# Cutting features as 128k + p in place of 4p + k in a chain of an RNN, a low-rank layer and an LSTM

## The chip, the cores and the metric

One NeuronCore of a Trainium2 chip runs the kernel. TensorE (PE) multiplies, VectorE (DVE) and ScalarE (ACT) do elementwise work, GpSimd (POOL) some reductions, SyncE (SP) issues DMAs; ScalarE issues a few too. The metric is the time of one execution on the device in microseconds.

## What is computed

Four layers with residuals, for 32 sequences (B) of 128 steps (T) and 512 features (D), in fp32. All layers but the second and fourth treat time steps alone; those two are recurrent, with 512 states.

```python
def reference(x, cond, ...):                      # x (32, 128, 512), cond (32, 512)
    ys = cond / sqrt(512)                         # layer 0: modulated linear
    d = rsqrt((ys * ys) @ (w0 * w0) + 1e-8)
    x = x + ((x * ys[:, None]) @ w0) * d[:, None]
    h = cond                                      # layer 1: RNN over t
    for t: h = tanh(h @ Wh1 + x[:, t] @ Wx1 + b1); x[:, t] += h
    ae = layernorm(cond) * ln_g + ln_b            # layer 2: low-rank hyper-network, rank 8
    xw = gelu(ae @ w1 + hb1) @ w2 + hb2           # 8192 values: a (512, 8) and b (512, 8)
    x = x + x @ (base + a @ b.T)
    h, c = cond, 0                                # layer 3: LSTM over t
    for t:
        i, f, o, g = split(x[:, t] @ Wx3 + b3 + h @ Wh3)
        c = sigmoid(f) * c + sigmoid(i) * tanh(g)
        h = sigmoid(o) * tanh(c)
        y[:, t] = x[:, t] + h
    return y
```

## The kernel before

**Data.** Features stand on the 128 partitions, in KC = 4 chunks (index k), with time and batch along the free side. Which feature stands where is set by `by_row` (L296): partition p, chunk k holds feature 4p + k, so each partition of a 512 x 512 weight is one stretch of 8 KB in memory. x, cond, b1 and the output come from arrays in the order 128j + p; `by_block` (L300) picks one j of them, and four DMAs, each to or from 32 partitions, move one tile (`load_x` L352, the stores L411, `condT` L612, `b1T` L374). On chip `columns` (L303) takes every fourth column where a chunk of output features is wanted: for the stationary operands of the dense products (`chunks` L1321), for the sources of the transposes in the LSTM step (L1034, L1037) and in a few operations of the start. `wh1` alone is put in order when it is split (`wh1_high` L495, `wh1_low` L808).

**Precision.** Each fp32 operand is split into a high and a low fp16 part (ScalarE's `high`, L477, and VectorE's `low`, L756), and a product is three fp16 products.

**The gates.** `wx3` and `wh3` come from memory with the columns of a row in the order (chunk j of 128 state features, gate g, feature in the chunk). A gate matmul (`gates_x` L1378, `gates_h` L1386) has a 128 x 32 stationary operand (state or input, all 32 sequences) and 512 moving weight columns; j = 0 to 3 go to four groups of 32 columns of the array, and to PSUM partitions 32j to 32j + 31. A step of the LSTM has 48 from x and 48 from h. The state leaves its elementwise work as 128 (j, b) x 128 features and is turned in blocks of 32 x 32 by VectorE (L1034 for the scaled fp16 copy that TensorE waits for, L1037 for the fp32 one).

**Order.** Every engine's order is written out by hand and kept by semaphores. Tiles have 4 time steps; the LSTM runs LAG = 2 tiles behind the RNN. TensorE's main loop (L1475) runs 30 rounds of four LSTM steps (`lstm`, `gates_x`), four RNN steps (`rnn`) and one tile of the dense products `l0`, `l1`, `z`, `x3_base`, `x3_low_rank`. After it come 8 LSTM steps with little beside them.

**The start.** SP issues `w0`, x tile 0, `wx1`, `wh1`, the hyper-network's `w1`, then the first four of 16 loads of w2 (`load_w2`, 1 MiB each, into the four slots of `ring`), x tiles 1 to 3, `b1T`, `wx3` in four loads, and then, as space comes free, w2 loads 4 to 7, `wh3` in four loads, `base`, w2 loads 8 to 15, and `b3`. ScalarE issues `condT`, `cond`, `ln_g`, `ln_b` and `hb1T` ahead of its own work; VectorE's LayerNorm waits for the last four of them together (L1069). `w2_unit(n)` on TensorE multiplies w2 load n and frees its slot. SP waits for `w2_used` before it issues n + 4. ScalarE sums squares of each `wx3` and `wh3` load as it lands (`wx3_squares`, `wh3_squares`), for their scales.

Of the kernel before, what the change touches and what calls it, by code (L numbers as in the profile page):

```python
# [5 lines left out]
P = 128  # L6
# [25 lines left out]
def build(nc, xT, condT, cond, w0, wx1, wh1, b1T, base, hw1, hb1T, hw2, hb2, ln_g, ln_b, wx3, wh3, b3, out):  # L32
# [8 lines left out]
    with ctx:  # L41
# [265 lines left out]
        def loaded_columns(w, oc):  # L307
            return w.rearrange("p (k q c) -> p k q c", k=KC, c=KC)[:, :, :, oc]
# [35 lines left out]
        def x_landed(engine, c):  # L344
            engine.wait_ge(ld_x[c % XT_RING], 16 * KC * (c // XT_RING + 1))

        @block.sync
        def _(sp):
# [25 lines left out]
            for j in range(KC):  # L374
                sp.dma_start(b1T_sb[FB * j:FB * j + FB], b1T.rearrange("(f k) j -> j f k", k=KC)[j],
                             allow_slow_non_contiguous=True).then_inc(ld_b1, 16)
# [23 lines left out]
            for j in range(KC):  # L400
                sp.dma_start(b3_sb[B * j:B * j + B], b3[j].partition_broadcast(B)).then_inc(ld_b3, 16)
# [3 lines left out]
            for i in range(LAG, TILES + LAG):  # L405
# [5 lines left out]
                for j in range(KC):  # L411
                    sp.dma_start(by_block(out[a].rearrange("p j t b -> p j (t b)"), j),
                                 x3T[a % 2][FB * j:FB * j + FB].rearrange("p k t b -> p k (t b)"))\
                      .then_inc(st_out[a % 2], 16)
            for q in range(2):
                sp.wait_ge(st_out[q], 16 * KC * TILES // 2)
# [58 lines left out]
        def _(act):  # L475
# [783 lines left out]
        def _(pe):  # L1259
# [61 lines left out]
            def chunks(w, oc):  # L1321
                return [columns(w[:, k])[:, oc] for k in range(KC)]
# [226 lines left out]
```

## Time and profile before

| | us |
|---|---|
| runs, median (lowest to highest of 3) | 1192.1 (1191.29 to 1196.86) |
| the profiled execution | 1191.93 |
| its span, first to last instruction | 1190.1 |
| TensorE busy | 1133.2 (95%) |
| VectorE busy | 911.4 (77%) |
| ScalarE busy | 425.3 (36%) |
| first gate matmul starts at | 107.16 |
| mean granted clock of TensorE | 0.987 |

Busy shares are means over stages that differ, so the page is read together with views that cut the time: the busy time of each engine in a stretch, the chain of work that ended last, and the order of instructions in a short window. A matmul's listed duration holds its pipeline; what it costs in a dense row is the distance to the next start.

### The profile page before, as it was taken

To read this page: it belongs to the slowest core of one execution; us is meant where nothing else is said; L and a number is where in the kernel's file an instruction comes from. 1 tells how busy PE (TensorE), PEld (TensorE's weight loads), DVE (VectorE), ACT (ScalarE), POOL (GpSimd) and SP (SyncE) were. 2 spreads that over 40 slices of the span, in tenths; PEclk is the share of its full clock that TensorE was granted. 3 is DMA by queue.
4 is the path that set the end of the run, shared out by engine and by line. 5 is a ranking of instruction groups with operands and counts; after the bars stand their busy time and mean duration, and the time that the engine had idled before them with its cause. 6 is when DMAs were issued, how large, how long until landed. Compare 5 with 4: busy or idle time off the path is not lost.

```text
span 1190.1 us, 50661 instructions
## 1 busy us (share of the span) xinstructions
PE 1133.2 (95%) x22740; PEld 756.6 (64%) x22740; DVE 911.4 (77%) x2645; ACT 425.3 (36%) x1032; POOL 56.2 (5%) x75
## 2 busy tenths in 40 slices
PE   2886999999999999999999999999999999999896
PEld 1653676667666766676677667766776677667542
DVE  4896777787777787877877778777787787777665
ACT  4794333333333332333333323333333233333221
POOL 1000000000000000000000000000000000000000
PEclk9987999999999999999999999999999999999998
DMA  9991000000000000000000000000000000000000
GB/s 323 388 347 42 3 21 20 21 20 21 20 13 10 21 21 21 20 21 20 12 12 21 20 20 21 21 21 11 13 20 21 20 21 21 11 10 5 12 11 19
DMA packets 49065, 51.00 MB, mean 43 GB/s; under 512 B 5984, under 2 KB 38752, under 8 KB 47184
## 3 DMA queue, kind: packets, MB, share of 16 engines
q1 hardware_dynamic: 47984, 47.50, 12.8%
q8 instruction: 178, 2.92, 1.0%
q10 hardware_dynamic: 864, 0.26, 0.1%
q14 instruction: 39, 0.32, 0.1%
HBM read 39.36 MB, written 8.39 MB: 40 GB/s over the span
## 4 chain that ended last, share of the span: by engine, by line
PE 90%; DVE 4%; ACT 2%; DMA 2%; issue 1%; ACTq 0%; DVEq 0%
PE ps_gates L1386 28%; PE ps_gates L1378 27%; PE ps_l L1317 14%; PE ps_x L1317 7%; PE ps_rnn L1402 6%; PE ps_rnn L1405 4%; PE ps_z L1317 2%; PE ps_lr L1317 2%; DMA ring<-in_hw 1%; PE ps_gates L1288 1%; DVE big L756 1%; DMA hb1T_sb<-in_hb1T 1%; ACT wh_hi L477 0%; DVE gates_ring L1012 0%; DVE late L1031 0%
## 5 line engine op out<-in xcount | busy, mean ns | idle before, releaser
L1386 PE MATMUL ps_gates<-big,lstm_h 128*32 128x512 f16 x6144 | 354.4, 379 | 4.4 <-DVE lstm_h L1034 4.4
L1378 PE MATMUL ps_gates<-big,rows 128*32 128x512 f16 x6144 | 345.8, 381 | 3.5 <-DVE rows L756 3.5
L1378 PEld LDWEIGHTS ps_gates<-big,rows 128*32 128x32 f16 x6144 | 165.3, 97 | 172.1 <-issue 6.6
L1386 PEld LDWEIGHTS ps_gates<-big,lstm_h 128*32 128x32 f16 x6144 | 158.1, 97 | 161.7 <-DVE lstm_h L1034 7.3
L599 ACT ACTIVATE gates_ring<-gates_ring 128x256 f32<-128x256 f32 x128 | 53.4, 418 | 337.9 <-DVE gates_ring L1012 337.9
L1012 DVE SCALAR_TENSOR_TENSOR gates_ring<-ps_gates,tile_un,rows 128x256 f32<-128x256 f32 x256 | 111.8, 477 | 68.3 <-PE ps_gates L1386 67.1
L1402 PE MATMUL ps_rnn<-rnn_h,wh_hi 128*128 128x64 f16 x2048 | 120.3, 192 | 6.9 <-DVE rnn_h L855 6.9
L1405 PE MATMUL ps_rnn<-rnn_h,wh_lo 128*128 128x32 f16 x2048 | 116.3, 177 | 0.0
L1402 PEld LDWEIGHTS ps_rnn<-rnn_h,wh_hi 128*128 128x128 f16 x2048 | 93.0, 96 | 35.3 <-issue 27.2
L1031 DVE SCALAR_TENSOR_TENSOR late<-gates_ring,tile_g,cell_tanh 128x128 f16<-128x128 f32 x128 | 45.0, 352 | 60.8 <-ACT cell_tanh L606 60.8
L1405 PEld LDWEIGHTS ps_rnn<-rnn_h,wh_lo 128*128 128x128 f16 x2048 | 91.2, 97 | 0.0
L1317 PE MATMUL ps_l<-xs,w_hi 128*128 128x128 f16 x1024 | 79.7, 222 | 2.1 <-DVE xs L756 1.9
L1317 PE MATMUL ps_l<-x,wx_hi 128*128 128x128 f16 x1024 | 79.3, 221 | 0.4 <-DVE x L756 0.4
L1317 PE MATMUL ps_x<-x,base_hi 128*128 128x128 f16 x1024 | 78.3, 219 | 0.0
L1317 PEld LDWEIGHTS ps_l<-xs,w_hi 128*128 128x128 f16 x1024 | 65.0, 114 | 3.2 <-DVE xs L756 2.0
L1317 PEld LDWEIGHTS ps_l<-x,wx_hi 128*128 128x128 f16 x1024 | 64.7, 114 | 1.4 <-issue 0.8
L1317 PEld LDWEIGHTS ps_x<-x,base_hi 128*128 128x128 f16 x1024 | 63.8, 114 | 0.4 <-issue 0.4
L592 ACT ACTIVATE x_ring<-rnn_pre 128x128 f32<-128x128 f32 x128 | 39.6, 310 | 64.6 <-DVE rnn_pre L849 64.6
L1037 DVE STREAM_TRANSPOSE lstm_hT<-lstm_h 128x128 f32<-128x128 f32 x128 | 53.5, 418 | 4.4
L477 ACT ACTIVATE x<-x_ring,tile_s 128x512 f16<-128x512 f32 x32 | 23.1, 722 | 84.8 <-DVE x_ring L860 84.8
L477 ACT ACTIVATE rnn_h<-x_ring,scales 128x128 f16<-128x128 f32 x128 | 51.5, 402 | 4.2
L606 ACT ACTIVATE cell_tanh<-cell 128x128 f32<-128x128 f32 x128 | 39.8, 311 | 33.0 <-DVE cell L1022 33.0
(181 smaller groups left out, 1560.2 us busy)
## 6 DMA issues: line engine op xcount, KB each, us to landing
ring<-in_hw SPq DMA_DIRECT2D x16, 1024.0 KB, 13.4
xT_sb<-in_xT SPq DMA_DIRECT2D x128, 64.0 KB, 2.4
outT<-late SPq DMA_DIRECT2D x128, 64.0 KB, 2.1
big<-in_wx SPq DMA_DIRECT2D x5, 1024.0 KB, 7.9
big<-in_wh SPq DMA_DIRECT2D x5, 1024.0 KB, 13.4
big<-in_w SPq DMA_DIRECT2D x1, 1024.0 KB, 5.8
big<-in_hw SPq DMA_DIRECT2D x1, 1024.0 KB, 11.8
late<-in_base SPq DMA_DIRECT2D x1, 1024.0 KB, 19.5
```

The costliest lines, as they stand in the source:

```text
L477: return nc.scalar.activation(out_, in_, ACT.Copy, scale=scale)
L592: nc.scalar.activation(h, rnn_pre[:], ACT.Tanh).then_inc(rnn_h_ready, 1)
L599: nc.scalar.activation(gates[:, 0:2 * P], gates[:, 0:2 * P], ACT.Sigmoid).then_inc(gates_acted, 1)
L606: nc.scalar.activation(cell_tanh[:], cell[:], ACT.Tanh).then_inc(cell_tanh_ready, 1)
L1012: nc.vector.scalar_tensor_tensor(gates[:, half], ps_gates[t % 2][:, half], tile_un[:, a, 0:1], b3_sb[:, half], ALU.mult, ALU.add).then_inc ...
L1031: nc.vector.scalar_tensor_tensor(lstm_hs, gates[:, 2 * P:3 * P], tile_g[:, following, 1:2], cell_tanh[:], ALU.mult, ALU.mult).then_inc(lst ...
L1037: nc.vector.transpose(lstm_hT[:], columns(lstm_h[:])).then_inc(lstm_hT_ready, 1)
L1317: last = nc.tensor.matmul(psum, w, x, start=(n == 0), stop=(n == len(triples) - 1))
L1378: nc.tensor.matmul(ps_gates[t % 2][B * j:B * j + B, :], x16[:, part, k, at:at + B], wx3_part(w_part, k)[:, GW * j:GW * j + GW], start=(n = ...
L1386: last = nc.tensor.matmul(ps_gates[t % 2][B * j:B * j + B, :], lstm_h16[:, part, k], wh3_part(w_part, k)[:, GW * j:GW * j + GW], start=Fal ...
L1402: nc.tensor.matmul(ps_rnn[:, at:at + 2 * B], wh1_hi[:, k, P * oc:P * oc + P], rnn_h16[:, k].rearrange("p h b -> p (h b)"), start=(k == 0), ...
L1405: last = nc.tensor.matmul(ps_rnn[:, at:at + B], wh1_lo[:, k, P * oc:P * oc + P], rnn_h16[:, k, 0], start=False, stop=(k == KC - 1))
```

## The change

Partition p, chunk k now holds feature 128k + p. So:

- x, `condT`, `b1T` and the output move in one DMA each, with 2 KB, 512 B, 16 B and 2 KB a partition; the semaphore counts follow.
- `w0`, `wx1`, `wh1`, `w1` and `base` (`by_row`) come as four stretches of 2 KB a partition. For `wx3` and `wh3`, which are loaded one k at a time, a partition still gets one stretch of 8 KB.
- Chunks of output features are neighbouring columns, in the dense products, the transposes and the start's operations. `wh1` is split in four pieces by k and not by output chunk.
- The 32 features of PSUM group j in chunk k are 128k + 32j + q. A gate matmul so takes its 512 moving columns as (gate, chunk k, 32 neighbours), 16 runs (`tile_columns`); PSUM columns are written in the order (gate, k, q) (`by_gate`).
- `b3` is laid out to match: 16 DMAs, one for each j and gate, with four stretches of 128 B a partition, in place of four DMAs with 2 KB a partition.

```diff
         def by_row(w):
-            return w.rearrange("(p k) n -> p k n", k=KC)
+            return w.rearrange("(k p) n -> p k n", k=KC)
-        def by_block(x, j):
-            return x.rearrange("(f k) j n -> j f k n", k=KC)[j]
-        def columns(x):
-            return x.rearrange("p (q c) -> p c q", c=KC)
+        def tile_columns(w, j):
+            return w.rearrange("p (k g j q) -> p j g k q", k=KC, g=GATES, q=B)[:, j]
+        def by_gate(x):
+            return x.rearrange("p (g k q) -> p g k q", g=GATES, q=B)
+        def by_chunk(x):
+            return x.rearrange("p (k q) -> p k q", q=B)
...
             def load_x(c):
-                for j in range(KC):
-                    sp.dma_start(xT_sb[c % XT_RING][FB * j:FB * j + FB].rearrange("p k t b -> p k (t b)"),
-                                 by_block(xT[c].rearrange("p j t b -> p j (t b)"), j)).then_inc(ld_x[c % XT_RING], 16)
+                sp.dma_start(xT_sb[c % XT_RING][:].rearrange("p k t b -> p (k t b)"),
+                             xT[c].rearrange("p j t b -> p (j t b)")).then_inc(ld_x[c % XT_RING], 16)
...
             for j in range(KC):
-                sp.dma_start(b3_sb[B * j:B * j + B], b3[j].partition_broadcast(B)).then_inc(ld_b3, 16)
+                for g in range(GATES):
+                    sp.dma_start(by_gate(b3_sb[B * j:B * j + B])[:, g],
+                                 b3.rearrange("k (g j q) -> g j k q", g=GATES, q=B)[g, j].partition_broadcast(B)).then_inc(ld_b3, 16)
...
-                for j in range(KC):
-                    sp.dma_start(by_block(out[a].rearrange("p j t b -> p j (t b)"), j),
-                                 x3T[a % 2][FB * j:FB * j + FB].rearrange("p k t b -> p k (t b)"))\
-                      .then_inc(st_out[a % 2], 16)
+                sp.dma_start(out[a].rearrange("p j t b -> p (j t b)"),
+                             x3T[a % 2].rearrange("p k t b -> p (k t b)")).then_inc(st_out[a % 2], 16)
...
-            def wh1_high(oc):
+            def wh1_high(k):
                 act.wait_ge(wh1_scale_ready, 1)
-                high(wh1_hi[:, :, P * oc:P * oc + P], loaded_columns(big[:, WH1_SLOT], oc), s_wh1).then_inc(wh1_hi_ready, 1)
+                high(wh1_hi[:, k], loaded(big[:, WH1_SLOT])[:, k], s_wh1).then_inc(wh1_hi_ready, 1)
...
-            for j in range(KC):
-                act.dma_start(condT_sb[FB * j:FB * j + FB], by_block(condT, j)).then_inc(ld_cond, 16)
+            act.dma_start(condT_sb[:], condT).then_inc(ld_cond, 16)
...
-            def wh1_low(oc):
-                dve.wait_ge(wh1_hi_ready, oc + 1)
-                low(wh1_lo[:, :, P * oc:P * oc + P], loaded_columns(big[:, WH1_SLOT], oc), s_wh1,
-                    wh1_hi[:, :, P * oc:P * oc + P]).then_inc(wh1_lo_ready, 1)
+            def wh1_low(k):
+                dve.wait_ge(wh1_hi_ready, k + 1)
+                low(wh1_lo[:, k], loaded(big[:, WH1_SLOT])[:, k], s_wh1, wh1_hi[:, k]).then_inc(wh1_lo_ready, 1)
...
-                nc.vector.transpose(lstm_h16[:, 0], columns(lstm_hs)).then_inc(lstm_hi_ready, 1)
+                nc.vector.transpose(lstm_h16[:, 0], by_chunk(lstm_hs)).then_inc(lstm_hi_ready, 1)
...
-                nc.vector.transpose(lstm_hT[:], columns(lstm_h[:])).then_inc(lstm_hT_ready, 1)
+                nc.vector.transpose(lstm_hT[:], by_chunk(lstm_h[:])).then_inc(lstm_hT_ready, 1)
...
             def chunks(w, oc):
-                return [columns(w[:, k])[:, oc] for k in range(KC)]
+                return [w[:, k, P * oc:P * oc + P] for k in range(KC)]
...
-                            nc.tensor.matmul(ps_gates[t % 2][B * j:B * j + B, :], x16[:, part, k, at:at + B],
-                                             wx3_part(w_part, k)[:, GW * j:GW * j + GW], start=(n == 0 and k == 0), stop=False,
+                            nc.tensor.matmul(by_gate(ps_gates[t % 2][B * j:B * j + B, :]), x16[:, part, k, at:at + B],
+                                             tile_columns(wx3_part(w_part, k), j), start=(n == 0 and k == 0), stop=False,
                                              tile_position=(0, B * j))
...
-                            last = nc.tensor.matmul(ps_gates[t % 2][B * j:B * j + B, :], lstm_h16[:, part, k],
-                                                    wh3_part(w_part, k)[:, GW * j:GW * j + GW], start=False,
+                            last = nc.tensor.matmul(by_gate(ps_gates[t % 2][B * j:B * j + B, :]), lstm_h16[:, part, k],
+                                                    tile_columns(wh3_part(w_part, k), j), start=False,
```

No compute instruction is added, taken away or moved on any engine. The lists of DMAs change. SP in the start, before (`big` holds the weights, `xT_sb` x, `x_ring` the bias of w2):

```order
L350 DMA big<-in_w 128x2048
L354 DMA xT_sb<-in_xT 32x4x128 x4
L350 DMA big<-in_wx 128x2048
L350 DMA big<-in_wh 128x2048
L350 DMA big<-in_hw 128x2048
L369 DMA x_ring<-in_hb 16x512
L360 DMA ring<-in_hw 128x4x512 x4
L354 DMA xT_sb<-in_xT 32x4x128 x12
L375 DMA b1T_sb<-in_b1T 32x4x1 x4
```

and the same stretch of SP's list now:

```order
L347 DMA big<-in_w 128x4x512
L350 DMA xT_sb<-in_xT 128x512
L347 DMA big<-in_wx 128x4x512
L347 DMA big<-in_wh 128x4x512
L347 DMA big<-in_hw 128x4x512
L365 DMA x_ring<-in_hb 16x512
L356 DMA ring<-in_hw 128x4x512 x4
L350 DMA xT_sb<-in_xT 128x512 x3
L370 DMA b1T_sb<-in_b1T 128x4
```

Nothing changes place; the tiles of x are one issue each. At the end of the start SP's list was, with `b3` as `rows`:

```order
L393 DMA late<-in_base 128x2048
L360 DMA ring<-in_hw 128x4x512 x8
L401 DMA rows<-in_b 32x512 x4
L354 DMA xT_sb<-in_xT 32x4x128 x8
L412 DMA outT<-late 128x1x128 x4
```

and is now:

```order
L387 DMA late<-in_base 128x4x512
L356 DMA ring<-in_hw 128x4x512 x8
L396 DMA rows<-in_b 32x4x32 x16
L350 DMA xT_sb<-in_xT 128x512 x2
L407 DMA outT<-late 128x512
```

The 16 issues of `b3` stand ahead of x tiles 4 and 5. ScalarE's list opened with

```order
L613 DMA condT_sb<-in_condT 32x4x32 x4
L614 DMA rows<-in_cond 32x512
L615 DMA rows<-in_ln_g 32x512
L616 DMA rows<-in_ln_b 32x512
L617 DMA hb1T_sb<-in_hb1T 128x4
```

and opens with

```order
L606 DMA condT_sb<-in_condT 128x128
L607 DMA rows<-in_cond 32x512
L608 DMA rows<-in_ln_g 32x512
L609 DMA rows<-in_ln_b 32x512
L610 DMA hb1T_sb<-in_hb1T 128x4
```

so `hb1T` stands behind four issues and not seven.

## Rows read from the trace of the kernel before

**Rows 1.** Busy us (x instructions) by engine, granted clock, DMA share, GB/s: rounds.

```profile
107.00:1124.00 1017.00, 1015.31 (x20928) 687.35 (x20929) 792.10 (x2334) 335.93 (x889) 47.05 (x56) 1.00 0.07 17
```

**Rows 2.** Chain of waits in one round (start us, us, what).

```profile
620.87 5.18 PE ps_gates L1378 x96
...
630.31 2.68 PE ps_l L1317 x48
```

**Rows 3.** TensorE's order in time (start us, us busy), rnn, a_hi and b_hi products.

```profile
613.76 0.22 PE L1317 MATMUL ps_lr<-zm,b_hi 128*128 128x64 f16 x2
...
614.46 0.61 PE L1317 MATMUL ps_l<-x,wx_hi 128*128 128x128 f16 x8
...
628.57 0.29 PE L1402 MATMUL ps_rnn<-rnn_h,wh_hi 128*128 128x64 f16 x4
628.69 0.26 PE L1405 MATMUL ps_rnn<-rnn_h,wh_lo 128*128 128x32 f16 x4
...
629.45 0.39 PE L1317 MATMUL ps_z<-x,a_hi 128*128 128x64 f16 x8
629.68 0.28 PE L1317 MATMUL ps_z<-x,a_lo 128*128 128x64 f16 x4
```

**Rows 4.** Chain of waits in the start.

```profile
5.07 9.57 DMA hb1T_sb<-in_hb1T
...
29.78 4.56 ACT wh_hi L477 x4
...
80.62 13.07 DMA ring<-in_hw
...
107.16 7.88 PE ps_gates L1378 x96
```

**Rows 5.** Order in time: condT's issues, squares of wh3(0), diagonal of base.

```profile
0.73 2.73 ACTq L613 DMA_DIRECT2D condT_sb<-in_condT  x4
...
60.20 1.90 ACT L480 ACTIVATE gates_ring<-big 128x2048 f16<-128x2048 f32 x1
...
69.70 1.32 DVE L923 SCALAR_TENSOR_TENSOR late<-ident,late 128x128 f32<-128x128 f32 x4
```

**Rows 6.** Groups: line, engine, operation, shapes, count | busy us, mean ns | idle before.

```profile
L477 ACT ACTIVATE wh_hi<-big,scales 128x512 f16<-128x512 f32 x4 | 4.7, 1245 | 0.0
...
L756 DVE SCALAR_TENSOR_TENSOR wh_lo<-big,scales,wh_hi 128x512 f16<-128x512 f32 x4 | 4.5, 1138 | 0.0
...
L477 ACT ACTIVATE x<-x_ring,tile_s 128x512 f16<-128x512 f32 x32 | 23.1, 722 | 84.8 <-DVE x_ring L860 84.8
...
L756 DVE SCALAR_TENSOR_TENSOR rows<-late,tile_g,rows 128x512 f16<-128x512 f32 x32 | 24.1, 752 | 27.2 <-ACT rows L477 27.2
...
L1034 DVE STREAM_TRANSPOSE lstm_h<-late 128x128 f16<-128x128 f16 x128 | 39.9, 312 | 4.4
```

**Rows 7.** Busy by engine; last two numbers DMA share, GB/s: 2 KB, 512 B, 8 KB pieces.

```profile
17.00:25.00 8.00, 5.03 (x24) 2.90 (x28) 5.51 (x26) 6.29 (x9) 2.63 (x5) 1.00 1.05 387
28.50:31.50 3.00, 2.75 (x22) 2.62 (x22) 3.00 (x4) 3.00 (x4) 0.00 (x0) 1.00 1.26 223
34.00:41.00 7.00, 5.20 (x37) 1.40 (x38) 6.86 (x11) 5.95 (x8) 0.00 (x0) 0.76 1.01 420
...
76.50:80.00 3.50, 3.50 (x40) 0.94 (x32) 3.47 (x9) 3.18 (x5) 0.00 (x0) 1.00 0.30 68
```

**Rows 8.** DMA issues in time, and us from issue to landing (base, last output).

```profile
47.96 0.43 SPq L393 DMA_DIRECT2D late<-in_base  x1
81.11 2.81 SPq L401 DMA_DIRECT2D rows<-in_b  x4
1185.73 2.50 SPq L412 DMA_DIRECT2D outT<-late  x4
...
late<-in_base SPq DMA_DIRECT2D x1, 1024.0 KB, 19.5
...
DMA to landing us min/median/max: 2.0/2.1/2.1
```

More of the change, by code:

```diff
@@ L344, in x_landed @@
         def x_landed(engine, c):
-            engine.wait_ge(ld_x[c % XT_RING], 16 * KC * (c // XT_RING + 1))
+            engine.wait_ge(ld_x[c % XT_RING], 16 * (c // XT_RING + 1))
         @block.sync
@@ L373, in _ @@
                 load_x(c)
-            for j in range(KC):
-                sp.dma_start(b1T_sb[FB * j:FB * j + FB], b1T.rearrange("(f k) j -> j f k", k=KC)[j],
-                             allow_slow_non_contiguous=True).then_inc(ld_b1, 16)
+            sp.dma_start(b1T_sb[:], b1T).then_inc(ld_b1, 16)
             for k in range(KC):
@@ L559, in b_high @@
                     act.wait_ge(b_ps, half + 1)
-                    high(b_hi[:, half].rearrange("p (q c) -> p q c", q=KC), columns(ps_b[half][:]), s_b).then_inc(b_hi_ready, 1)
+                    high(b_hi[:, half], ps_b[half][:], s_b).then_inc(b_hi_ready, 1)
             def zm_high(a):
@@ L610, in lstm @@
                 lstm_tanh(t)
-            for j in range(KC):
-                act.dma_start(condT_sb[FB * j:FB * j + FB], by_block(condT, j)).then_inc(ld_cond, 16)
+            act.dma_start(condT_sb[:], condT).then_inc(ld_cond, 16)
             act.dma_start(ln_rows[:, 0], cond).then_inc(ld_rows, 16)
@@ L921, in base_diagonal @@
                 for k in range(KC):
-                    own = columns(late[:, D * k:D * k + D])[:, k]
+                    own = late[:, D * k + P * k:D * k + P * k + P]
                     nc.vector.scalar_tensor_tensor(own, ident[:], 2.0, own, ALU.mult, ALU.add).then_inc(base_ready, 1)
@@ L974, in b_low @@
                     dve.wait_ge(b_hi_ready, half + 1)
-                    low(b_lo[:, half].rearrange("p (q c) -> p q c", q=KC), columns(ps_b[half][:]), s_b,
-                        b_hi[:, half].rearrange("p (q c) -> p q c", q=KC))\
-                        .then_inc(b_lo_ready, 1)
+                    low(b_lo[:, half], ps_b[half][:], s_b, b_hi[:, half]).then_inc(b_lo_ready, 1)
             def x2_low(a):
@@ L997, in x3 @@
                 dve.wait_ge(tile_un_ready, a + 1)
-                wait(dve, st_out[a % 2], 16 * KC * (a // 2))
+                wait(dve, st_out[a % 2], 16 * (a // 2))
                 dve.wait_ge(base_ps, a + 1)
@@ L1127, in _ @@
             xs(1)
-            dve.wait_ge(ld_b1, 16 * KC)
+            dve.wait_ge(ld_b1, 16)
             xw1(0)
@@ L1197, in _ @@
             gate_scales(1)
-            dve.wait_ge(ld_b3, 16 * KC)
+            dve.wait_ge(ld_b3, 16 * KC * GATES)
             dve.wait_ge(sq_ready, 4 + 2 * KC)
@@ L1297, in turn_a @@
                             at = P * (2 * k + q)
-                            last = nc.tensor.transpose(ps_turned[n][:, at:at + P], columns(a_rows[:, q])[:, 2 * n + k], ident[:])
+                            last = nc.tensor.transpose(ps_turned[n][:, at:at + P], a_rows[:, q, P * (2 * n + k):P * (2 * n + k) + P], ident[:])
                     last.then_inc(a_ps, 1)
@@ L1412, in _ @@
             for k in range(KC):
-                last = nc.tensor.transpose(ps_z[:, B * k:B * k + B], columns(ae)[:, k], ident[0:B, 0:B])
+                last = nc.tensor.transpose(ps_z[:, B * k:B * k + B], ae[:, P * k:P * k + P], ident[0:B, 0:B])
             last.then_inc(aeT_ps, 1)
@@ L1418, in _ @@
             pe.wait_ge(dsum_moved, 1)
-            unfolded(ps_rnn, lambda k: columns(folded)[:, k]).then_inc(dsum_ready, 1)
+            unfolded(ps_rnn, lambda k: folded[:, P * k:P * k + P]).then_inc(dsum_ready, 1)
             pe.wait_ge(ld_w1, 16)
```

6 lines of the change are left out of this document (2 added, 4 removed).

## The prediction

> **What bounds the kernel now.** I read the stage view first. From 107 us to 1124 us TensorE is busy 1015.3 of 1017 us at a granted clock of 1.00, while VectorE is busy 792 and ScalarE 336 [rows 1]: there the time is TensorE's alone, 30 rounds of some 34 us. Before 107 us is the start, after 1124 the tail, and these have limits of their own.
>
> In a round the chain of waits holds nothing but matmuls. 96 gate matmuls of 512 columns take 5.18 us [rows 2], which is 216 ns for each four that run side by side on four column groups; per column that is 0.42 ns, one column at 2.4 GHz. 48 dense matmuls of 128 columns take 2.68 us [rows 2], 55.9 ns each, so the same column time and some 2.5 ns.
>
> In the start the chain opens with a DMA of 2 KB, `hb1T`, which is issued at 5.07 us and lands 9.57 us later [rows 4]. LayerNorm waits for it, and everything on VectorE and ScalarE up to the first gate matmul at 107.16 hangs behind it, through the split of `wh1` on ScalarE (4.56 us) and the last hyper-network weights (`ring`), for which TensorE waits until 93.7 [rows 4]. The DMA engines are full meanwhile: 387 to 420 GB/s [rows 7].
>
> **The change, part by part.**
>
> *The gates' moving columns.* A gate matmul reads its 512 columns as 16 runs of 32 in place of one run. Matmuls, loads, order and output columns stay as they are in number. No row shows four such streams at once, so I bound it. The product with `a_hi` reads 64 columns as four runs of 16: 8 of them take 0.23 us from one start to the next (629.45 to 629.68), 29 ns each; the recurrence reads 64 columns in one run, and 4 take 0.12 us, 30 ns each [rows 3]. A run's end therefore costs nothing that this trace can show. The upper bound is one column time for each run: 16 x 0.42 = 6.7 ns in 216. There are 12,288 gate matmuls, 3072 groups of four, so +20.5 us. I take 0, since the row with runs is a single stream but otherwise the same operation, and price the rest as a rival.
>
> *Stationary operands of the dense products* (`w0`, `wx1`, `base`) come from neighbouring columns, where now they take every fourth. Their matmuls are at the column time already (55.9 ns for 128 columns), so a faster load saves nothing; the load would have to be what binds, and then 128 columns would not stand on the line through 64 columns (29) and 512 (216). 0, and a gain is nearly excluded.
>
> *Splitting `wh1`.* Four pieces with every fourth column take 1245 ns each on ScalarE and 1138 on VectorE; pieces of the same size with neighbouring columns take 722 and 752 [rows 6]. On ScalarE the four lie on the chain, 4.56 us, and become 4 x 0.72 = 2.9: -1.7 us. VectorE's saving (1.5 us) lies beside it.
>
> *ScalarE's DMA queue.* `condT` took four issues, 2.73 us [rows 5]; one costs some 0.6, so that `hb1T` is issued 2.1 us sooner. It carries 2 KB and flew for 9.57 us; it was waiting beside the 1 MiB weight loads of the other queue, whose pieces shrink from 8 KB to 2 KB. So it lands 2.1 us sooner at least, and perhaps 7. I take 5: LayerNorm starts at 9.7, the `wh1` split ends 5 + 1.7 = 6.7 us sooner, and so does what follows, until a DMA is late. The Trainium skill, DMA: Bandwidth & Descriptors, section Queues, rings and completion order, says that an engine takes turns between queues by packets, which would favour the larger end; nothing in the sum rests on it.
>
> *The DMA engines themselves.* x in pieces of 512 B moves at 223 GB/s, 2 KB pieces at 387, 8 KB pieces at 420 [rows 7]. A tile of x (256 KiB) so goes from about 1.2 us to 0.7, and with `b1T`'s single floats gone too I take -2.6 us for four tiles (-2.0 by the rates alone). The four early weights (1 MiB each) go from 2.50 to 2.71 us: +0.8. So the `wh3` loads land 1.8 us sooner, `base` 1.6.
>
> *What is late next.* `base` was issued at 47.96 and took 19.5 us, landing at 67.4; `wh3(0)` landed four loads of 2.5 us before it, at 57.4 [rows 8]. With the change they land at 55.6 and 65.8. ScalarE would want `wh3(0)` at 60.20 - 6.7 = 53.5 [rows 5] and waits until 55.6: the lead shrinks to 4.6. VectorE would want `base` at 69.70 - 4.6 = 65.1 [rows 5]: 0.7 of waiting, and the lead is 3.9 us. The ring loads 12 to 15 are issued as TensorE frees slots, so they move by the same 3.9: the queue ran nearly dry before them (68 GB/s from 76.5 to 80 us [rows 7]), so there is room. The last lands at 89.8 in place of 93.7, and the first gate matmul starts at 103.3. **Start: -3.9 us.** Ends: -1.7, if only the `wh1` split counts; -4.7, where the dry stretch of the queue is used up.
>
> *`b3` in 16 DMAs.* SP issued four in 2.81 us [rows 8], so 16 take 11 us. Behind them on SP stand x tiles 4 and 5; ahead of them is only the last ring load. Issued from about 77 to 88, `b3` lands by some 90 and is first waited for after 103. Free, as long as that cover of 13 us stands. At a quarter of the rate of the x tiles, an estimate for their pieces of 128 B beside 512 B, the 256 KiB would take 5 us of the 13. The Trainium skill, DMA: Bandwidth & Descriptors, Specifications, wants at least 512 B a piece for full rate, which would leave the sum as it is.
>
> *Transposes in the LSTM step.* VectorE's transposes read neighbouring columns now. In the rounds that is hidden behind TensorE. In the tail the fp16 one (312 ns [rows 6]) lies on the chain 8 times. The nearest price of a stride is `wh1`'s, (1138 - 752) / 512 = 0.75 ns an element or 97 ns for 128; that source is fp32, with a step of 16 bytes where the transpose has 8, so I take 30 ns: **-0.3 us**, between 0 and -0.9.
>
> *Small operands in the start* (the diagonal of `base`, the turned a, b, LayerNorm's transposes) lose their strides in operations of which there are 2 to 4 each: 0, 0.1 us at most either way.
>
> *The output.* After the last VectorE operation SP issues four DMAs, 2.50 us from 1185.73, and each lands 2.0 to 2.1 after its issue [rows 8]. One issue leaves 1.9 us out, and its 256 KiB need 0.7 us against 0.3 for the last 64 KiB: **-1.5 us**, between -1.0 and -1.9. The stores and loads inside the rounds are off the path.
>
> *Sum*: -3.9 - 0.3 - 1.5 = -5.7 us. The profiled execution took 1191.9 us (span 1190.1), so 1186.2; the median of the runs is 0.2 above it: **1186.4 us**.
>
> **The rivals.**
>
> *Rival 1: runs cost column time (slower).* At each of the 16 runs the stream loses one column, with four streams reading one another's neighbourhood: +20.5 us, 1206.9. It decides from 5.7 us / 3072 = 1.9 ns a group, 0.9% of 216. For it: no row has four streams with runs. Against it: the `a_hi` row, single stream, no loss. The Trainium skill, SBUF — State Buffer, section Door 1: The DMA port swizzle, says that each access crossing to a new 16-byte line pays a penalty; a run of 32 fp16 is four whole lines, so by it nothing is added. PSUM — Partial Sum Buffer, Specifications, says that any non-contiguous pattern there slows matmuls significantly; the `ps_lr` products write four runs of 16 and 24 of them take 0.70 us (613.76 to 614.46) [rows 3], 29 ns each, so the trace does not agree.
>
> *Rival 2: the ScalarE queue gains nothing.* `hb1T` lands near its old time because the start of w0 delays both queues alike. Then only the `wh1` split moves the start: -1.7 - 0.3 - 1.5 = -3.5, 1188.6. For it: the first loads on an idle queue are slow too. Against: the issue alone is 2.1 sooner.
>
> *Rival 3: the start follows further.* The lead is limited only where the queue's dry stretch is used up (-4.7), transposes give 0.9, the store 1.9: -7.5, 1184.6.
>
> *Rival 4: the dense products gain.* Neighbouring columns in the loads bring their 4608 matmuls from 55.9 to the bare 53.3 ns of 128 columns: -12 us more, 1174. Against it: the recurrence's loads are as large, read neighbouring columns, and its matmuls show the same 2 to 3 ns above their column time [rows 3].
>
> **How the numbers follow.** My forecast has 0.45, rival 1 0.13, rival 2 0.20, rival 3 0.20, rival 4 0.01, something else 0.01. The forecast's own spread is 1184.9 to 1188. From 1182.5 to 1190.5 the range holds the forecast and rivals 2 and 3 with their bounds, some 0.84; rival 1 is left out. Half a per cent is 6.0 us, about what a measurement tells from no change, so "faster" begins at 1186.1, in the middle of my forecast: 0.2 of its 0.45, rivals 3 and 4, together 0.42 faster; the rest of it and rival 2, 0.45 within; 0.13 slower.
>
> **What would show it.** In the rounds: 96 gate matmuls in 5.18 us; 5.34 us for 96 would be rival 1. LayerNorm's first operation near 9.7 us (rival 2: near 14.7). `wh1`'s four pieces at 0.72 us. ScalarE waiting some 2 us for a `wh3` load. The first gate matmul near 103.3. Fp16 transposes under 312 ns. One output DMA, landing about 2.5 us after its issue. The forecast is wrong if a gate group takes over 218 ns, if `b3` is waited for, or if the start is not shorter by 2 to 5 us.

## The result, and the profile after

The changed kernel takes 1183.2 us (median; 1181.6 to 1183.5), the one before in the same comparison 1191.4 us. The medians differ by 8.3 us, 0.7%; the ratio of the runs is 0.9915 with a 95% interval of 0.9894 to 0.9936. The forecast was 1186.4 us and leaned slightly to "within half a per cent". The time lies in its range, near the low end, but the gain was forecast as 5.7 us and is beyond half a per cent.

The profiled execution has a span of 1181.5 us, 8.6 less than before. The stage view of the rounds (columns as in [rows 1]):

```profile
107.00:1124.00 1017.00, 1014.13 (x20988) 687.38 (x20984) 774.27 (x2336) 336.79 (x892) 46.98 (x56) 1.00 0.05 17
```

TensorE is as full as in [rows 1], at the same clock. The chain of waits in a round (start us, us, what):

```profile
512.65 5.18 PE ps_gates L1368 x96
517.83 2.59 PE ps_gates L1376 x48
```

96 gate matmuls take 5.18 us as in [rows 2]: 216 ns for four, with moving columns in runs of 32. The period of two LSTM steps is 17.005 us where it was 17.017, so the rounds give 0.7 us (60 such periods).

The chain of waits in the start, which answers [rows 4]:

```profile
2.91 6.59 DMA hb1T_sb<-in_hb1T
...
45.47 19.08 DMA late<-in_base
64.57 0.90 DVE late L915 x4
65.47 0.67 DVE x L749
66.19 5.30 PE ps_l L1307 x48
...
72.75 3.62 PE ps_gates L1278 x32
76.38 11.91 DMA ring<-in_hw
...
101.75 7.51 PE ps_gates L1368 x91
```

`hb1T` lands at 9.50 us in place of 14.65. `base` lands at 64.55 in place of 67.44, and now VectorE stands there and waits for it (1.05 us). The last ring load lands at 88.29 in place of 93.69, and the first gate matmul starts at 101.75 in place of 107.16: the start gives 5.4 us. The first gates take 0.4 us less too: TensorE's granted clock stays at 0.50 for some 4.4 us behind the first gate matmul, and for 5.1 in the kernel before. In the tail the span ends 3.4 us after the last fp32 transpose of the state begins, where it was 5.5: 2.0 us. Together 5.4 + 0.4 + 0.7 + 2.0 = 8.5 us.

The single operations, grouped (columns as in [rows 6]):

```profile
L1027 DVE STREAM_TRANSPOSE lstm_hT<-lstm_h 128x128 f32<-128x128 f32 x128 | 39.9, 311 | 4.4
L1024 DVE STREAM_TRANSPOSE lstm_h<-late 128x128 f16<-128x128 f16 x128 | 39.8, 311 | 4.4
...
L749 DVE SCALAR_TENSOR_TENSOR wh_lo<-big,scales,wh_hi 128x512 f16<-128x512 f32 x4 | 2.9, 748 | 0.0
...
L471 ACT ACTIVATE wh_hi<-big,scales 128x512 f16<-128x512 f32 x4 | 2.6, 714 | 0.0
```

The fp16 transpose costs what it did (311 and 312 ns): its stride was free. The fp32 one falls from 418 to 311 ns. SP's issues at the end of the start, and the last one of the output:

```profile
73.81 2.94 SPq L356 DMA_DIRECT2D ring<-in_hw  x4
76.86 11.93 SPq L396 DMA_DIRECT2D rows<-in_b  x16
...
1179.07 0.33 SPq L407 DMA_DIRECT2D outT<-late  x1
```

The 16 issues of `b3` take 11.93 us (11 were reckoned); `b3` has landed at 91 and nothing waits for it.

### The profile page after: what moved, and what is told of

It is laid out like the page before. It is cut to its first block, busy times and chain, and to the rows that moved or that the text cites. A ratio compares the mean times of both kernels' runs of the same rounds, so it can differ in the third digit from the quotient of the medians.

```text
span 1181.5 us, 50475 instructions
## 1 busy us (share of the span) xinstructions
PE 1131.5 (96%) x22740; PEld 757.0 (64%) x22740; DVE 890.7 (75%) x2645; ACT 423.2 (36%) x1032; POOL 55.4 (5%) x75
## 4 chain that ended last, share of the span: by engine, by line
PE 90%; DVE 4%; DMA 3%; ACT 1%; issue 1%; SPq 1%; ACTq 0%; DVEq 0%
PE ps_gates L1376 28%; PE ps_gates L1368 27%; PE ps_l L1307 14%; PE ps_x L1307 7%; PE ps_rnn L1392 6%; PE ps_rnn L1395 4%; PE ps_z L1307 2%; PE ps_lr L1307 2%; DMA late<-in_base 2%; DMA ring<-in_hw 1%; DMA hb1T_sb<-in_hb1T 1%; PE ps_gates L1278 0%; SPq L386 0%; DVE big L749 0%; DVE gates_ring L1002 0%
## 5 line engine op out<-in xcount | busy, mean ns | idle before, releaser
L1307 PEld LDWEIGHTS ps_x<-x,base_hi 128*128 128x128 f16 x1024 | 61.4, 98 | 0.4 <-issue 0.4
L1307 PE MATMUL ps_l<-xs,w_lo 128*128 128x128 f16 x512 | 50.7, 223 | 0.0
```

The lines of the kernel that those rows point to most:

```text
L1307: last = nc.tensor.matmul(psum, w, x, start=(n == 0), stop=(n == len(triples) - 1))
```

## The experiments

Two ideas were to be told apart for the start. **A**: two chains meet at `base`, the LayerNorm chain (`hb1T`, splits, TensorE) and the DMA queue, and the later one counts. **B**: the LayerNorm chain is all. Each part was undone alone first. "First gate" is the start of the first gate matmul in the profiled execution, against 101.75; times are medians, against 1183.2. In several of these runs values stand in another order or come from other columns than the layers want; the number and shapes of the compute operations stay.

**condT in four DMAs (e1_cond4).**

```
-            act.dma_start(condT_sb[:], condT).then_inc(ld_cond, 16)
+            for k in range(KC):
+                act.dma_start(condT_sb[:, k], condT[:, k]).then_inc(ld_cond, 16)
```

> The changed kernel with condT in four DMAs on ScalarE's queue again (128 B a partition each). Theory A (two chains meet at base: VectorE waited 1.05 us for base, which lands at 64.55, so the LayerNorm chain has that much slack): hb1T is issued some 1.5 to 2 us later and lands that much after 9.50; base lands where it did, and the diagonal of base starts 0.5 to 1.0 us after 64.57, the first gate matmul 0.5 to 1.0 after 101.75; time +0.7 us. Theory B (only the LayerNorm chain counts, transfers are hidden): the first gate matmul moves by all of it, +1.5 to +2. Theory C (hb1T lands by the other queue's load, not by its own issue): it lands at 9.5 as before, +0.

Measured: 1183.2 us, first gate 102.40. Its chain:

```profile
4.77 7.73 DMA hb1T_sb<-in_hb1T
...
43.24 4.50 PE ps_l L1308 x48
```

`hb1T` is issued 1.9 us later and lands 3.0 later (12.50), the diagonal of `base` starts 1.6 later, and of that 0.65 us reach the first gate matmul and nothing measurable the time. B falls, and so does C, since the landing moved. A is right in kind, and its 0.5 to 1.0 us at the first gate matmul came out, but partly by luck: `hb1T` came later than A had it, and then 1.6 us shrank to 0.65. What shrinks them is in the chain rows: 48 products of `ps_l` after `base` take 5.30 us in the changed kernel and 4.37 here. In both TensorE had waited just before, and its granted clock was 0.50 from 62 to 72 us there and from 64 to 71 here.

**x and b1T in four DMAs (e2_x4).** Each tile as `xT_sb[:, k]` from `xT[c][:, k]` for k = 0 to 3, `b1T` by its columns.

> The changed kernel with each tile of x in four DMAs of 512 B pieces and b1T in four DMAs of single floats. Theory A (the DMA engines are the bound up to base): b1T lands 2.6 us later (33.0), base at 66.8 to 67.4, VectorE waits for it, and the last ring load comes another 1 us later for x tiles 4 and 5 in small pieces; first gate matmul 2.3 to 3.8 us after 101.75. Theory B (LayerNorm chain alone): hb1T lands where it did, first gate matmul within 0.5 us of 101.75.

Measured: 1184.4 us, first gate 104.75, `base` at 67.33 (+2.8), and VectorE waits 1.07 us for it. A, though the profiled execution was the slowest of its four: by the medians x and `b1T` are worth 1.2 us, by the profile 3.0.

**wh1 split with strides (e4_wh1).**

```
-                high(wh1_hi[:, k], loaded(big[:, WH1_SLOT])[:, k], s_wh1)
+                high(wh1_hi[:, :, P * k:P * k + P], every_fourth(k), s_wh1)
```

> The changed kernel with wh1 split from every fourth column again (four pieces by column, written side by side; the columns of wh1 so stand in another order and the RNN's values are not the reference's). Each piece takes 1245 ns on ScalarE and 1138 on VectorE in place of some 722 and 752. Theory A (1.05 us of slack at base): ScalarE ends the split 2.0 us later, the diagonal of base starts about 1.0 us later, first gate matmul +1.0. Theory B (all of it on the path): +2.0. If the path left ScalarE elsewhere before: 0.

Measured: 1184.1 us, first gate 102.38. The pieces cost 1216 and 1163 ns, the diagonal starts 1.8 us later, w2_unit(8) 0.5 us later: the clock again gives back part.

**x tiles 4 and 5 ahead of b3 (e3_x_first).**

> The changed kernel with the 16 DMAs of b3 issued behind x tiles 4 and 5 instead of ahead of them. In the changed kernel the last ring load took 11.91 us from issue, in the one before 13.07, and x tile 4 was issued only after it had landed. Theory D (the 12 us of b3's issues hold x tiles 4 and 5 back, which otherwise take their turns with the ring loads): the last ring load lands 0.5 to 1.3 us later than 88.29 and the first gate matmul moves by as much. Theory E (that flight became shorter for another reason): ring load 15 within 0.2 us of 88.29, no change in time. Neither expects the loop to wait for b3.

Measured: 1182.5 us, first gate 100.61, the last ring load at 87.05. D has the wrong sign. But most of that is not the place of `b3`: the three ring loads ahead of the last are issued 1.1 us sooner (the last itself 0.3 later), because TensorE freed their slots sooner. The diagonal starts 0.3 us later than in the changed kernel, and then

```profile
66.49 4.20 PE ps_l L1308 x48
```

the 48 products take 4.20 us, not 5.30. Runs whose start is that of the changed kernel, with `b3` in its old place, show the same scatter: w2_unit(8) starts between 71.4 and 72.7 us, the first gate matmul between 100.8 and 102.0. One of them, e8_dense below, frees the slots as soon as this run does, and has its last ring load at 87.42 and the first gate matmul at 100.88. So the place of `b3` is worth some 0.3 us at most, which one profile doesn't settle.

**The output in four DMAs, one for each k, to all 128 partitions (e5_out4).**

> The changed kernel with each output tile in four DMAs, one for each chunk (64 KiB, 512 B a partition). In the tail of the changed kernel the span ends 3.4 us after the last fp32 transpose of the state, in the kernel before 5.5. Theory A (the four issues on SP are the difference): SP's last four issues take 2.5 us again and the span ends 1.9 to 2.0 us later after that transpose; nothing else moves: time +1.9. Theory B (the bytes or the landing are the difference): under +1.

Measured: 1184.3 us, between A and B. The last issues are

```profile
1178.85 1.96 SPq L408 DMA_DIRECT2D outT<-late  x4
```

and the span ends 4.6 us after the transpose, 1.2 more than with one DMA. Of the 2.0 us gained, 1.2 come from issuing once. The rest goes with the form before, to 32 partitions each: its four issues took 2.50 us and not 1.96, its DMAs landed 2.1 us after issue and not 1.6, and the fp32 transpose took 0.1 more.

**Other moving columns for the gates (e6_runs_c_8, e7_runs_2_1, e12_runs_4_s2).** `tile_columns` replaced, here for runs of 8 (q is the run length; the x products of e6_runs_c_8 take one run, the h products of e12_runs_4_s2 every second column of a stretch of 1024), by

```
+            return w.rearrange("p (a j q) -> p j a q", j=KC, q=8)[:, j]
```

> The changed kernel with other moving columns for the gates (their weights no longer belong to the gates that the step wants, so values differ): the products from x take 512 columns in one run and write PSUM in one run, the products from h take 512 columns as 64 runs of 8 columns (16 B) with gaps of 24, PSUM written in the same order. Theory A (TensorE reads a column each 0.42 ns whatever the run): both stay at 216 ns for four matmuls, 0 in time. Theory B (a run's end costs a column time, hidden in the runs of 32 by something): the x products fall below 216, the h products rise, by 64 x 0.42 = 27 ns a group of four, 1536 groups: +41 us.

> As the run before it, but the products from x take 256 runs of 2 columns (4 B, gaps of 6 columns) and those from h 512 single columns, every fourth (8 B apart). Theory A (a column each 0.42 ns whatever the run): 216 ns for four in both, time unchanged. Theory C (a read pays for each new stretch of 16 or more bytes that it touches): the x products touch a new 16 B with each run of 2, the h products with every second column, so a group costs up to double, 1536 x 216 ns for each kind: up to +330 us each.

> The changed kernel with other moving columns for the gates (values differ): products from x take 128 runs of 4 columns (8 B, gaps of 12 columns, 24 B), products from h take 512 single columns, every second one (4 B apart). So far: runs of 8 columns (16 B) and longer 216 ns for four, runs of 2 columns 16 B apart and single columns 8 B apart both some 450. Theory G (a read brings a stretch of some bytes, and the rate is that of the stretches touched; a stretch of 8 B): runs of 4 stay at 216, every second column has 4 B of 8 unused and needs 512 / 2 stretches, two columns each, at the rate of a stretch a column: 216. Theory H (any gap inside 16 B halves the rate): every second column 450, and runs of 4, 8 B of each 32, 450 as well.

Measured: 1183.0, 1912.9 and 1222.8 us. The bursts in the chain of waits, e7_runs_2_1 and then e12_runs_4_s2 (some matmul records are missing, so counts are short; a burst is 96 or 48):

```profile
500.87 10.94 PE ps_gates L1374 x88
511.81 5.48 PE ps_gates L1382 x44
```

```profile
509.68 5.51 PE ps_gates L1374 x96
...
532.87 2.72 PE ps_gates L1382 x48
```

For four matmuls of 512 columns, gates from x and gates from h apart:

| moving columns | stretches of 16 B touched, by one matmul | ns for four |
|---|---|---|
| one run; 16 runs of 32; 64 runs of 8 | 64 | 216 |
| 128 runs of 4 | 128 | 5510 / 24 = 230 |
| every second column | 128 | 2720 / 12 = 227 |
| 256 pairs, 16 B apart | 256 | 10940 / 24 = 456 |
| every fourth column | 256 | 5480 / 12 = 457 |

Runs of 8 columns and more are free; A holds that far, and B falls. Runs of 4 and every second column cost 5 to 6%; pairs and every fourth column cost double. G fails on the pairs, which touch as many stretches of 8 B as every second column does; H is wrong about the cheap ones; C has the right thing that is counted, the stretches of 16 B. All five kinds stand on one line: 456 / 256 = 1.78 ns for each stretch, 128 of them 228 ns, and 64 of them 114, which the column time of 213 covers. That line was drawn after the runs and not tried on a further one, and what in the chip sets it is not shown. The Trainium skill, SBUF — State Buffer, section Door 1: The DMA port swizzle, says that accesses need at least 2 hits in a line of 16 bytes for full rate; here 2 columns a line run at half rate and 4 at 94%, so for four matmuls side by side the measurement asks for more.

**Dense operands with strides (e8_dense).**

```
-                return [w[:, k, P * oc:P * oc + P] for k in range(KC)]
+                return [w[:, k].rearrange("p (q c) -> p c q", c=KC)[:, oc] for k in range(KC)]
```

> The changed kernel with the stationary operands of the dense products from every fourth column again (w0, wx1 and base; the output features so stand in another order and the values differ). The kernel before lost 11 ns more where the first eight base products of a step start (455 against 444 ns), once a step. Theory A (that is the load of strided columns showing where no matmul covers it): 455 again, the rounds 0.7 us longer, the rest of the dense products at 55.9 ns. Theory B (something else, such as the order of operands in memory): 444 stays, 0.

Measured: the period is 17.015 us (17.017 before, 17.005 changed), and the first eight base products behind the recurrence's, once a round, take 454 ns again, not 443. Two other places where a row of dense products begins give 2.5 ns each. A: the dense operands are the 0.7 us of the rounds. The loads themselves show it. In the kernel before, and then in the changed one,

```profile
L1317 PEld LDWEIGHTS ps_l<-x,wx_hi 128*128 128x128 f16 x1024 | 64.7, 114 | 1.4 <-issue 0.8 <-DVE x L756 0.5
```

```profile
L1307 PEld LDWEIGHTS ps_l<-x,wx_hi 128*128 128x128 f16 x1024 | 63.2, 99 | 2.6 <-issue 1.3 <-DVE x L749 1.3
```

a load of every fourth column is listed with 114 ns, of neighbouring columns with 99; in e8_dense it is 114 again. The median, 1182.8, is within scatter.

**The kernel before with condT last (e9_before_cond_last).**

> The kernel before with condT's four DMAs moved behind hb1T on ScalarE's queue; all else, x in 512 B pieces and the strided wh1 split included, as it was. Theory A (two chains meet at base): hb1T is issued near 2.3 us and lands near 9.5, the LayerNorm chain wants base's diagonal 5 us sooner (64.6), but base lands at 67.4, or at 66.3 if w2 loads 4 to 7 follow the sooner TensorE: first gate matmul 2.3 to 3.4 us before 107.16; time -2.3 to -3.4. Theory B (the LayerNorm chain is all): first gate matmul -5.

Measured: 1194.7 us beside 1192.8 of the kernel before, ratio 1.002 (1.0006 to 1.0035): slower. Its chain opens with

```profile
5.03 10.07 DMA condT_sb<-in_condT
```

`hb1T` and the rows landed at 8.7 us, as both theories had it, but a step of VectorE beside LayerNorm needs `condT` (L1065), which now is last and lands at 15.1. Which DMA is last doesn't matter; when the last of the eight lands does. The `wh1` split starts 1.0 us later than before (30.7), the first gate matmul 3.8 later (110.91). Nearly all of the rest is TensorE at its lower clock: 48 products that took 2.88 us in the kernel before take 4.44 (granted clock 0.50 at 50 to 52 us, where it was 1.00), and 48 later ones 5.31 in place of 4.28, together 2.6 us.

**The early weights in 8 KB pieces (e13_w8k).**

```
-                sp.dma_start(big[:, slot].rearrange("p (k n) -> p k n", k=KC), by_row(w))
+                sp.dma_start(big[:, slot], w.rearrange("(p k) n -> p (k n)", k=KC))
```

> The changed kernel with w0, wx1, wh1 and w1 loaded as one stretch of 8 KB a partition (rows 4p to 4p + 3 on partition p again, so the values differ). hb1T lands at 9.50 in the changed kernel, at 14.65 in the one before, and condT in four explains 3.0 of it. Theory P (the two queues take turns at the DMA engines packet by packet, so each small packet of ScalarE's queue waits for one of the other queue's, 8 KB or 2 KB): hb1T lands near 11.6 though issued at 2.9, VectorE reaches base's diagonal 1.0 us later, first gate matmul +0.4 to +1.0. Theory Q (pieces of the other queue don't matter): hb1T within 0.5 us of 9.5, 0.

Measured: 1182.2 us, first gate 100.36.

```profile
3.03 8.94 DMA hb1T_sb<-in_hb1T
...
42.72 2.85 PE ps_l L1307 x48
```

`hb1T` lands at 11.97, 2.5 us later, as P has it. But P's first gate matmul, 0.4 to 1.0 us later, is 1.4 sooner. The diagonal still starts when `base` lands (64.14, itself 0.4 sooner): these 48 products, 4.50 us in e1_cond4 at a granted clock of 0.50, kept the full clock, and the 48 behind `base` are shorter than in the changed kernel too. With `hb1T` 0.5 us sooner than in e1_cond4, VectorE was in time.

**All undone but b3 (e14_all_but_b3), x and b1T kept in one (e15_only_x), and all with narrow DMAs (e18_old_start).**

> The changed kernel with all of the start's edits undone but b3 and the operands' order in small operations: condT in four, x and b1T in four each, the early weights and base in 8 KB pieces, wh1 split with strides (values differ). If the parts found are all there is: hb1T near 14.7, base near 67.4, its diagonal near 69.7, the first gate matmul 106 to 107.2, time 1188.5 to 1189.7 (the output's 2.0 and the rounds' 0.7 stay gained). If something is missing: first gate matmul under 105.5.

> As e14_all_but_b3, but x and b1T in one DMA each as in the changed kernel. Theory A (two chains meet at base, and the later one sets the time): base lands 2.6 us sooner than in e14 but VectorE reaches its diagonal no sooner, since the LayerNorm chain is late: diagonal within 0.4 us of e14's, first gate matmul 0 to 1.2 us sooner than e14's (1.2 if the x tiles beside the last ring load count). Theory S (the gains add): 3.0 us sooner than e14, as x gave when undone alone.

> As e14_all_but_b3, but the DMAs of x, condT and b1T in the form of the kernel before: each of the four to 32 partitions, with four pieces a partition (512, 128 and 4 B), in place of one piece to each of 128 partitions. Theory N (narrow DMAs are slower, and the 2.2 us are theirs): ring load 3 lands near 28.4 and b1T near 33.1 (e14: 26.91, 30.91), hb1T near 14.6 (13.07), base near 67.4 (65.90), the first gate matmul at 106.3 to 107.2, time +2 from e14's 1185.95. Theory M (the rest is b3 and the small operands, or the scatter of TensorE's clock): landings as in e14 within 0.3 us.

Measured: 1186.0, 1190.0 and 1188.7 us, first gate 104.97, 110.74 and 107.58. e14's is under the 105.5 that was to tell that a part is missing; e18_old_start adds the narrow form (each DMA to 32 partitions). The chains of e14, e15 and e18 open with

```profile
4.48 8.59 DMA hb1T_sb<-in_hb1T
```

```profile
4.91 11.97 DMA hb1T_sb<-in_hb1T
```

```profile
5.03 8.59 DMA hb1T_sb<-in_hb1T
```

With x in one DMA but the rest as before, the kernel is 4 us slower than with x in four. `base` lands at 69.6, 3.7 us later than in e14: TensorE frees the ring's slots late and the queue waits for it (20, 0 and 70 GB/s in the three stretches of 2 us from 38 us on). Neither A nor S had that. `hb1T` lands at 16.9. The five loads of ScalarE's queue hold 46 packets for each of 16 DMA engines when `condT` has pieces of 128 B (32 of them `condT`'s), and 22 when it has 512 B, counted from the shapes. Last landings by these two numbers:

| | weights in 2 KB | weights in 8 KB |
|---|---|---|
| condT in 512 B | 9.5 to 10.4 | 12.0 |
| condT in 128 B | 12.5 | 16.9 (13.1 with x in 512 B beside it) |

Turn by turn with SP's packets this comes out in kind: the delays behave like products of count and size, not like sums (2.5 + 3.0 would give 15.0), and small packets of x in between go with a shorter one. The turns themselves are argued from these landings. The Trainium skill, DMA: Bandwidth & Descriptors, section Queues, rings and completion order, says that an engine takes turns between queues by packets; these runs agree, though that page's packet may hold several pieces and the count here is of pieces.

The narrow form is the last part. GB/s is the last number; the stretch 28 to 30 us, x tiles nearly alone, of e18_old_start (512 B to 32 partitions), e14_all_but_b3 (512 B to 128) and the changed kernel (2 KB to 128):

```profile
28.00:30.00 2.00, 1.89 (x17) 1.76 (x18) 2.00 (x4) 2.00 (x3) 0.00 (x0) 1.00 1.40 231
```

```profile
28.00:30.00 2.00, 2.00 (x20) 2.00 (x21) 2.00 (x3) 2.00 (x3) 0.00 (x0) 1.00 1.25 302
```

```profile
28.00:30.00 2.00, 1.78 (x26) 0.77 (x23) 1.86 (x6) 0.92 (x2) 0.00 (x0) 1.00 1.09 409
```

N: x tiles 1 to 3 and `b1T` take 4.9, 4.0 and 2.2 us, and the narrow form costs 2.6 us of the first gate matmul. The medians differ by 2.7, but come from two comparisons whose intervals overlap (0.9923 to 0.9961 and 0.9945 to 0.9979). The first gate matmul is now at 107.58, where the kernel before has 107.16. That they agree so well is partly luck: beside the kernel before, `hb1T` lands 1.0 us sooner, the fourth ring load 0.9 sooner, `base` 0.5 later, and its diagonal starts 2.0 later, behind 48 products that took 4.42 us and not 2.88. So the start is accounted for to a microsecond or so. `b3` in four DMAs was not tried.

**base ahead of wh3(3) (e10_base_early), with two more orders (e11_best), and again beside the changed kernel (e16_after_again, e17_base_early_again).**

```
                 else:
                     sp.wait_ge(u_parts, 1)
+                    sp.dma_start(late[:].rearrange("p (k n) -> p k n", k=KC), by_row(base)).then_inc(ld_base, 16)
                 sp.dma_start(wh3_staged(k), by_row(wh3)[:, k]).then_inc(ld_wh3[k], 16)
-            sp.dma_start(late[:].rearrange("p (k n) -> p k n", k=KC), by_row(base)).then_inc(ld_base, 16)
```

> The changed kernel with base loaded ahead of wh3's last quarter. It lands near 62.0 in place of 64.55, before VectorE wants it (63.5), and wh3(3) at 64.5, which ScalarE wants at 63.65. Theory A (base's landing is what the chain waits for): the diagonal starts 1.05 us sooner, first gate matmul 1.0 sooner. Theory F (TensorE's granted clock takes it back: the runs with wh1 and condT changed had the diagonal 1.6 to 1.8 us later and w2_unit(8) only 0.4 to 0.5 later, for 48 products took 4.3 us and not 5.3): w2_unit(8) and the first gate matmul move by under 0.5.

> The changed kernel with three orders changed: base ahead of wh3's last quarter, condT last on ScalarE's queue (hb1T issued 0.5 us sooner), b3's 16 DMAs behind x tiles 4 and 5. Theory A (each is on the path): 1.05 to 1.5 from base and hb1T, 1.2 from b3 (as its run alone), first gate matmul near 99.3, time -2.4. Theory F (granted clock takes the first part back): -1.2 from b3 alone, first gate matmul near 100.6.

> The changed kernel itself, beside the next run: 1183.2 us, first gate matmul 100.9 to 102.0.

> base ahead of wh3's last quarter, beside the run before it. Theory A: 1181.2 us, 2 us less, with the first gate matmul near 99.8 and w2 loads 12 to 15 following one another without a gap. Theory F (the gain of e10 was a lucky granted clock): within 0.7 us of the run before it.

Measured: 1181.2, 1182.3, and side by side 1182.9 (1182.87 to 1183.36) and 1181.7 (1181.51 to 1182.72). `base` lands at 61.9, the diagonal starts at 63.4, w2_unit(8) at 69.5 and the first gate matmul at 99.8. TensorE frees the slots so soon that the ring's loads follow one another at 2.7 us: the queue is the bound. The gain beside the changed kernel is 1.2 us, 0.1%, every run under every run of the other; the intervals of their ratios to the kernel before (0.9891 to 0.9921 and 0.9901 to 0.9930) overlap, so it is small at best: less than A's 2 us and more than F's 0.7. The two more orders add nothing: with `condT` last it lands at 11.2 and the chain starts there.

## Why the prediction was right or wrong

**The gates' runs: 0, right.** 5.18 us for 96. The upper bound of a column time for each run was far off for runs of 32; a loss begins only at runs of 4. Rival 1 fell, and rival 4 holds for 0.7 us of its 12.

**Dense operands: 0, missed by 0.7 us.** A strided operand takes 14 to 15 ns longer to load. Inside a row of products that changes nothing; where a row begins it costs up to 11 ns once a round and 2.5 ns twice. [rows 2] average over 48 products, and hide it. That the load is longer stands in the trace of the kernel before (114 ns, where the unstrided loads of the recurrence have 96).

**wh1: right in size** (714 and 748 ns), but of the 1.7 us that it leaves on ScalarE only some 0.6 reach the first gate.

**hb1T: right, 9.5 where 9.7 was forecast**, and for the reason given: issued sooner, and beside smaller pieces. The two are not separate terms. Rival 2 fell.

**base at 65.8: wrong, 64.55.** This step failed, in its terms and not in its kind. It was to come 1.6 us sooner and came 2.9 sooner. Single landings mislead here: in the kernel before, ring load 7 landed 3.9 us behind the one ahead of it, the others 2.7, though the DMA engines moved 386 to 425 GB/s all the while. The bytes of all DMA packets, added up in order of time, tell where the changed kernel got ahead. At 8.8 MB (near the end of the fourth ring load) it led by 0.1 us, behind x tiles 1 to 3 and `b1T` (10.4 MB) by 2.5, from 15.2 MB to `base` by 2.6 to 2.8. The terms, beside those of the forecast:

- 2 KB pieces in the early weights: +0.8 was forecast. With them in 8 KB pieces again (e13_w8k) the same bytes are moved 0.35 us sooner and `base` lands 0.4 sooner, so they cost about +0.4 (between runs that share the changed start the same bytes scatter by 0.3 us).
- x and `b1T`: -2.6 was forecast, -2.4 came from tiles 1 to 3 and `b1T` and some -0.4 from tile 0 (the lead of 0.1 although the weights cost 0.35): -2.8.
- The queue's waits for ring slots 4 to 7 were put at nothing. In the kernel before, the last of these loads was issued at 45.57 us, 2.5 us behind the landing of the last `wx3` load, and the DMA engines moved less around it. With the sooner LayerNorm chain it is issued at 37.10, 3.9 us ahead of that landing, and the loss is gone: -0.3 us. The stretches, of the kernel before and of the changed one (GB/s last):

```profile
40.00:42.00 2.00, 2.00 (x22) 0.56 (x15) 2.00 (x4) 1.89 (x2) 0.00 (x0) 0.85 0.94 351
44.00:46.00 2.00, 2.00 (x38) 1.07 (x36) 1.21 (x5) 0.00 (x0) 0.00 (x0) 1.00 1.01 350
```

```profile
40.00:42.00 2.00, 1.78 (x26) 1.78 (x27) 0.41 (x2) 1.97 (x5) 0.00 (x0) 0.82 1.05 387
44.00:46.00 2.00, 2.00 (x46) 1.59 (x43) 1.28 (x2) 0.82 (x3) 0.38 (x1) 0.82 1.02 382
```

I had looked for the queue's dry stretch at 76 to 80 us alone. These come to -2.7. What is left, with `base`'s own 2 KB pieces (+0.2 forecast) in it, is within scatter: `base` lands between 64.5 and 65.1 us in the runs that share this start.

**What is late next: half right.** ScalarE waits 0.7 us for `wh3(0)` where 2 were forecast (2.0 in e16_after_again, the same kernel), VectorE 1.05 for `base` where 0.7 were. The lead past `base` is 5.1 us, not 3.9.

**"They move by the same 3.9": wrong in form.** Behind `base` the lead went down to 4.2 by TensorE's half clock (5.30 us for 48 products, before 4.28) and up to 5.4 in the last ring load's flight (11.91 us, before 13.07). What of that flight belongs to `b3` and what to x tiles is not told apart.

**b3: free, right**, on the cover named.

**Transposes: -0.3, and it was 0** for fp16. The price of `wh1`'s stride (4 floats) doesn't carry to a transpose of fp16; it carries to the fp32 one (97 ns reckoned, 107 measured), which I had left out of the tail: 0.1 us.

**Output: -1.5, and it was -1.9** of the tail's 2.0, at the edge of its bounds; the other 0.1 is the transpose. The single DMA of 256 KiB lands 2.0 us after its issue, as one of 64 KiB did [rows 8]; I had added 0.4 for its bytes.

Sum: 5.4 + 0.4 in the start and behind it against 3.9, 0.7 against 0, 2.0 against 1.5, 0 against 0.3. The mechanisms stand; the start's term was too small, above all by `base`, 1.3 us. Rival 3 (the start follows further, 1184.6) is nearest to what happened, but by luck: it had the lead limited at the dry stretch of 76 to 80 us alone, and `base` still limited it, as VectorE's wait of 1.05 us shows. The chance of "faster" was too low, because its edge lay in the middle of my forecast and all errors of the sum but the transposes' went one way.

## What to carry to other kernels

Undo parts in groups as well as alone. Three parts of this change are worth 0 to 3 us alone, and one of them costs 4 us where the others are missing, as small packets of one queue then stand beside large ones of another. Where two chains meet, look for every place at which the DMA queue waits for a slot, and not for the emptiest one, and count the bytes moved by a given time rather than landings; and price a write to memory by its issue and one landing, not by its bytes.

## What the runs showed of the hardware that was not expected

- In a start full of waits, the stretches that TensorE spends at the lower of its two granted clocks move the end by 1 us between runs whose start is the same code: the 48 products behind `base` took 4.20 to 5.30 us. Elsewhere 48 products took 2.85 us at the full clock, and 4.50 at a granted clock of 0.50 in a run whose chain was 0.5 us later. It damps some delays (1.6 us became 0.65) and amplifies others (1.0 us became 3.8).
- Moving operands of fp16 are read at a column in 0.42 ns down to runs of 16 B; with four matmuls side by side each new stretch of 16 B that one of them touches takes 1.78 ns, so that 4 columns a stretch cost 5 to 6% more time and 2 columns double.
- A stationary operand of every fourth fp16 column loads in 114 ns, of neighbouring columns in 98 to 100; only where a row of products begins does it show, as 2.5 to 11 ns.
- In the stretch from 28 to 30 us, DMAs to 32 partitions with four pieces each move at 231 to 233 GB/s, to 128 partitions with pieces of the same 512 B at 302, with 2 KB at 409.
